# Half of each product with B moved to GpSimd behind a ScalarE copy, and all four batches in one straight block

## The reference, cut to what matters

```
def step(h, ts):
    dt, B_t, C_t, x_t = ts
    dA = jnp.exp(A[None] * dt[:, :, None])
    dBx = dt[:, :, None] * B_t[:, None, :] * x_t[:, :, None]
    h = dA * h + dBx
    y = jnp.einsum('bdn,bn->bd', h, C_t) + D * x_t
    return (h, y)
...
y = y * jax.nn.silu(z)
y = y @ out_proj_w.T + out_proj_b
r = y + residual
```

## Time and profile before

| | |
|---|---|
| median of 3 runs | 2946.02 us (2938.42 to 2959.98) |
| the profiled execution | 2938.01 us, span 2936.2 us |
| scan stage, first ScalarE instruction of the block to the last residual | 1283.7 to 1622.4 us, 338.7 us |
| busy in the whole span | PE 76%, DVE 60%, ACT 35%, POOL 23% |
| mean granted TensorE clock | 0.845 of full speed |

### The profile page before, as it was taken

How to read it: one execution, slowest core, us unless ns; L and a number is a source line. 1 busy time by engine, 2 the same in 40 slices (tenths; PEclk the granted TensorE clock), 3 DMA queues, 4 the chain that set the end, 5 groups by cost and what they waited for, 6 DMA issues and landing times. The chain is left out here.

```text
span 2936.2 us, 37724 instructions
## 1 busy us (share of the span) xinstructions
PE 2233.7 (76%) x12210; PEld 1461.8 (50%) x12210; DVE 1761.6 (60%) x4110; ACT 1034.3 (35%) x2220; POOL 687.5 (23%) x1221
## 2 busy tenths in 40 slices
PE   2579699995999784546666599398489868999688
PEld 1245588882555444212222355287334346776577
DVE  2546566674675455789898554554689655556422
ACT  0135222220564451444343134322157723344222
POOL 0033244431110420124354232134111000000121
PEclk8669799996796797778788589599779979999799
DMA  7032000003110410000000321000411000000000
GB/s 282 0 99 52 1 1 0 0 0 100 44 51 15 106 40 0 0 0 0 0 0 0 110 49 35 1 1 0 136 37 44 23 36 1 0 0 0 1 0 14
DMA packets 58426, 93.92 MB, mean 32 GB/s; under 512 B 11264, under 2 KB 31040, under 8 KB 57152
## 3 DMA queue, kind: packets, MB, share of 16 engines
q0 software_dynamic: 29952, 36.45, 5.1%
q1 hardware_dynamic: 27488, 45.67, 4.7%
q10 hardware_dynamic: 864, 10.30, 0.9%
HBM read 65.63 MB, written 31.29 MB: 33 GB/s over the span
## 5 line engine op out<-in xcount | busy, mean ns | idle before, releaser
L815 DVE TENSOR_REDUCE m<-bank 128x1 f32<-128x512 f32 (+3 forms) x512 | 272.4, 583 | 77.4 <-PE bank L968 50.2
L1235 DVE TENSOR_REDUCE m<-bank 128x2 f32<-128x308 f32 x384 | 164.3, 475 | 203.8 <-PE bank L1507 118.1
L2322 PEld LDWEIGHTS bank<-w_ffn,eh 128*128 128x128 f32 x2144 | 276.5, 191 | 20.0
L2322 PE MATMUL bank<-w_ffn,eh 128*128 128x128 f32 x2144 | 278.7, 275 | 0.0
L2311 PE MATMUL bank<-x_hi,w_hi 128*128 x472 | 217.3, 460 | 71.0 <-POOL w_lo L2239 55.0
L936 ACT ACTIVATE p<-bank 128x512 f32<-128x512 f32 (+3 forms) x512 | 234.0, 522 | 97.6 <-PE bank L1014 58.7
L2661 PE MATMUL bank<-hc,w_start 128*128 128x512 f32 x256 | 162.0, 766 | 102.7 <-POOL hc L2609 102.6
L2592 DVE TENSOR_TENSOR_SCAN sh<-dA,dbx 128x512 f32<-128x512 f32 x128 | 218.2, 1743 | 2.2
L966 PE MATMUL bank<-K,Qf 32*128 32x512 f32 (+2 forms) x512 | 180.8, 507 | 37.9 <-PEq L330 33.1
L2237 POOL CAST w_hi<-w_ffn 128x256 fp32r<-128x256 f32 (+1 forms) x256 | 95.0, 371 | 482.3 <-SPq L2227 325.1
L2609 POOL TENSOR_TENSOR hc<-sh,cb 128x1024 f32<-128x1024 f32 x64 | 152.1, 2377 | 199.9 <-DVE sh L2592 151.0
(11 more groups left out here) (399 smaller groups left out, 4587.5 us busy)
## 6 DMA issues: line engine op xcount, KB each, us to landing
Qf<-stack_q_plain POOLq DMA_DIRECT2D x48, 256.0 KB, 3.0
Qf<-stack_q_masked POOLq DMA_DIRECT2D x32, 256.0 KB, 3.0
K<-stack_k_self POOLq DMA_DIRECT2D x32, 256.0 KB, 3.1
w_ffn<-ffn_dram ACTq DMA_DIRECT2D x1, 6144.0 KB, 33.5
stack_q_plain<-q_hi SPq DMA_DIRECT2D x24, 256.0 KB, 3.4
stack_q_masked<-q_hi SPq DMA_DIRECT2D x16, 256.0 KB, 3.0
stack_k_self<-k_hi SPq DMA_DIRECT2D x16, 256.0 KB, 3.1
K<-stack_k_ctx POOLq DMA_DIRECT2D x48, 80.0 KB, 2.6
```

Source lines behind the costliest of these rows:

```text
L815: ins = dve.reduce_max(k.m[:, t, h:h + 1], bank[:, 0:(t + 1) * P if k.kind == "page" else S], AX)
L1235: dve.reduce_max(k.m[:, t:t + 2, h], first_banks[c % 3][:].rearrange("p (a k) -> p a k", a=2)[:, :, 0:S2], AX).then_inc(sem("max_done"), 1)
L2322: last = pe.matmul(bank[:, t * P:(t + 1) * P], k.h[:, n % RING, t * P:(t + 1) * P], w(down.format(e))[:, i * P:(i + 1) * P], start=(i == 0 ...
```

## The change

- dbx is cut in two. VectorE makes half 0 (L2590 of the changed kernel), GpSimd makes half 1 (`second_dbx`, L2615). Both read B from a new SBUF tile bb, double buffered, which ScalarE copies from the bank (`copy_B`, L2638). TensorE's next spread into a B bank waits for that copy, no longer for dbx.
- VectorE's second scan of a step waits for GpSimd's half. GpSimd issues `second_dbx(u + 2)` behind the product hc of step u. ScalarE issues `copy_B(u + 1)` ahead of the two exponentials of step u.
- dtx is double buffered by batch and made at step 8 of the batch before (`weigh`, two 512-column products).
- The loop is gone: one straight block of 64 steps over all four batches.

```diff
-        self.dtx = sb("dtx", [P, 2, S])
+        self.dtx = sb("dtx", [P, 2, 2, S])
+        self.bb = sb("bb", [P, 2, S])
...
-    steps = BODY * NSTATE
+    steps = B * NSTATE
...
+            def weigh(e):
+                for i in range(2):
+                    last = dve.tensor_tensor(k.dtx[:, e % 2, i], k.xc[:, e, i], k.dt[:, e], ALU.mult)
+                last.then_inc(sem("dtx_ready"), 1)
+                dve.wait_ge(sem("dtx_ready"), e + 1)
+
+            weigh(0)
             for u in range(steps):
                 e, s = divmod(u, NSTATE)
-                if s == 0:
-                    dt = k.dt[:, bass.ts(b0 + e, 1), :]
-                    xc = k.xc[:, bass.ts(b0 + e, 1)].rearrange("p o i q -> p (o i) q")
-                    ch.link(dve.tensor_tensor(k.dtx[:], xc, dt.to_broadcast([P, 2, S]), ALU.mult))
-
-                dve.wait_ge(sem("B_done"), u + 1)
-                dve.tensor_tensor(k.dbx[:, u % 2], k.dtx[:], over(ps[u % 2][:], 1, 2), ALU.mult).then_inc(sem("dbx_ready"), 1)
-                dve.wait_ge(sem("dbx_ready"), u + 1)
+                if s == 8 and e + 1 < B:
+                    weigh(e + 1)
+
+                dve.wait_ge(sem("B_ready"), u + 1)
+                dve.tensor_tensor(k.dbx[:, u % 2, 0], k.dtx[:, e % 2, 0], k.bb[:, u % 2], ALU.mult).then_inc(sem("first_dbx"), 1)
+                dve.wait_ge(sem("first_dbx"), u + 1)
                 for i in range(2):
+                    if i == 1:
+                        dve.wait_ge(sem("second_dbx"), u + 1)
                     dve.wait_ge(sem("dA_ready"), 2 * u + i + 1)
...
         @block.gpsimd
         def _(pool):
+            def second_dbx(u):
+                e = u // NSTATE
+                if u % NSTATE == 0:
+                    pool.wait_ge(sem("dtx_ready"), e + 1)
+                pool.wait_ge(sem("B_ready"), u + 1)
+                nc.gpsimd.tensor_tensor(k.dbx[:, u % 2, 1], k.dtx[:, e % 2, 1], k.bb[:, u % 2], ALU.mult).then_inc(sem("second_dbx"), 1)
+
+            second_dbx(0)
+            second_dbx(1)
             for u in range(steps):
...
                 nc.gpsimd.tensor_tensor(k.hc[:, u % 2], k.h[:, u % 2], over(k.cb[:, u % 2], 1, 2), ALU.mult).then_inc(sem("hc_ready"), 1)
+                if u + 2 < steps:
+                    second_dbx(u + 2)
...
+            def copy_B(u):
+
+                act.wait_ge(sem("B_done"), u + 1)
+                if u >= 2:
+                    act.wait_ge(sem("first_dbx"), u - 1)
+                    act.wait_ge(sem("second_dbx"), u - 1)
+                nc.scalar.copy(k.bb[:, u % 2], ps[u % 2][:]).then_inc(sem("B_ready"), 1)
+
+            copy_B(0)
             for u in range(steps):
                 e, s = divmod(u, NSTATE)
+                if u + 1 < steps:
+                    copy_B(u + 1)
...
                 if u >= 2:
-                    pe.wait_ge(sem("dbx_ready"), u - 1)
+                    pe.wait_ge(sem("B_ready"), u - 1)
...
-            with nc.Fori(0, B // BODY, 1) as i:
-                scan_block(net, i * BODY, k)
+            scan_block(net, k)
             scan_finish(net, k)
```

More of the change, by code:

```diff
@@ L53 @@
 LN_BN = 6
-BODY = 2
 GROUP = 4
@@ L2548, in scan_prepare, with scan_block @@
     end_of_block(net)
-def scan_block(net, b0, k):
+def scan_block(net, k):
     nc, sem, ps, w = net.nc, net.sem, net.ps, net.w
-    steps = BODY * NSTATE
+    steps = B * NSTATE
     with nc.Block() as block:
@@ L2567, in apply_gate @@
                 for i in range(2):
-                    last = dve.tensor_tensor(k.g[:, i], ps[4 + 2 * (e % 2) + i][:], k.zs[:, bass.ts(b0 + e, 1), i].rearrange("p o q -> p (o q)"), ALU.mult)
+                    last = dve.tensor_tensor(k.g[:, i], ps[4 + 2 * (e % 2) + i][:], k.zs[:, e, i], ALU.mult)
                 last.then_inc(sem("gated_ready"), 1)
@@ L2573, in residual @@
                 dve.wait_ge(sem("out_done"), e + 1)
-                xn = k.n.xn[:, bass.ts(b0 + e, QT), :]
+                xn = k.n.xn[:, e * QT:(e + 1) * QT, :]
                 dve.tensor_tensor(xn, ps[4 + 2 * (e % 2)][:].rearrange("p (t d) -> p t d", t=QT), xn, ALU.add).then_inc(sem("r_ready"), 1)
+            def weigh(e):
[4 more added lines that the diff above has]
+            weigh(0)
             for u in range(steps):
                 e, s = divmod(u, NSTATE)
-                if s == 0:
-                    dt = k.dt[:, bass.ts(b0 + e, 1), :]
-                    xc = k.xc[:, bass.ts(b0 + e, 1)].rearrange("p o i q -> p (o i) q")
-                    ch.link(dve.tensor_tensor(k.dtx[:], xc, dt.to_broadcast([P, 2, S]), ALU.mult))
-                dve.wait_ge(sem("B_done"), u + 1)
-                dve.tensor_tensor(k.dbx[:, u % 2], k.dtx[:], over(ps[u % 2][:], 1, 2), ALU.mult).then_inc(sem("dbx_ready"), 1)
-                dve.wait_ge(sem("dbx_ready"), u + 1)
+                if s == 8 and e + 1 < B:
[3 more added lines that the diff above has]
+                dve.wait_ge(sem("first_dbx"), u + 1)
                 for i in range(2):
+                    if i == 1:
+                        dve.wait_ge(sem("second_dbx"), u + 1)
                     dve.wait_ge(sem("dA_ready"), 2 * u + i + 1)
@@ L2596, in _ @@
                     residual(e - 1)
-            apply_gate(BODY - 1)
-            residual(BODY - 1)
-            dve.wait_ge(sem("r_ready"), BODY)
+            apply_gate(B - 1)
+            residual(B - 1)
+            dve.wait_ge(sem("r_ready"), B)
         @block.gpsimd
         def _(pool):
+            def second_dbx(u):
[6 more added lines that the diff above has]
+            second_dbx(1)
             for u in range(steps):
@@ L2609, in _ @@
                 nc.gpsimd.tensor_tensor(k.hc[:, u % 2], k.h[:, u % 2], over(k.cb[:, u % 2], 1, 2), ALU.mult).then_inc(sem("hc_ready"), 1)
+                if u + 2 < steps:
+                    second_dbx(u + 2)
+            pool.wait_ge(sem("hc_ready"), steps)
         @block.scalar
         def _(act):
+            def copy_B(u):
[5 more added lines that the diff above has]
+            copy_B(0)
             for u in range(steps):
                 e, s = divmod(u, NSTATE)
+                if u + 1 < steps:
+                    copy_B(u + 1)
                 for i in range(2):
@@ L2618, in _ @@
                         act.wait_ge(sem("h_ready"), 2 * (u - 2) + i + 1)
-                    dt = k.dt[:, bass.ts(b0 + e, 1), :].rearrange("p o q -> p (o q)")
-                    nc.scalar.activation(k.dA[:, u % 2, i], dt, ACT.Exp, scale=k.A[:, i * NSTATE + s:i * NSTATE + s + 1]).then_inc(sem("dA_ready"), 1)
+                    nc.scalar.activation(k.dA[:, u % 2, i], k.dt[:, e], ACT.Exp, scale=k.A[:, i * NSTATE + s:i * NSTATE + s + 1]).then_inc(sem("dA_ready"), 1)
                 act.wait_ge(sem("C_done"), u + 1)
@@ L2630, in spread @@
                 e, s = divmod(u, NSTATE)
-                bc = k.bc[:, bass.ts(b0 + e, S)]
+                bc = k.bc[:, e * S:(e + 1) * S]
                 if u >= 2:
-                    pe.wait_ge(sem("dbx_ready"), u - 1)
+                    pe.wait_ge(sem("B_ready"), u - 1)
                 pe.matmul(ps[u % 2][:], w("sel")[:, s * P:(s + 1) * P], bc, start=True, stop=True).then_inc(sem("B_done"), 1)
@@ L2657, in _ @@
                     for i in range(2):
-                        pe.matmul(ps[4 + 2 * (e % 2) + i][:], k.D[:, i, :], k.xc[:, bass.ts(b0 + e, 1), i].rearrange("p o q -> p (o q)"), start=True, stop=False)
+                        pe.matmul(ps[4 + 2 * (e % 2) + i][:], k.D[:, i, :], k.xc[:, e, i], start=True, stop=False)
                 pe.wait_ge(sem("hc_ready"), u + 1)
@@ L2664, in _ @@
                     output(e - 1)
-            output(BODY - 1)
+            output(B - 1)
     end_of_block(net)
```

## The result

The changed kernel takes 3020.76 us (median of 4 runs, 3005.65 to 3024.09) against 2942.22 us before; the ratio is 1.0249 with an interval of 1.0189 to 1.0309. Five further rounds of the same kernel gave 1.0262 (1.0240 to 1.0284), the narrower figure; one of their six executions took 5126 us, which nothing on record explains, and is left out of that ratio. The changed kernel is slower, as forecast, and lies 7 us under the predicted 3028 us, inside the range of 3000 to 3065.

A forecast was written before the change was run, and what follows sets the result against it. VectorE instructions with two SBUF operands and GpSimd products were taken to exclude each other, bounding the step. Terms +95.8 − 15.2 + 1.7 + 2.4 + 1.5 = +86.2 us gave 3024 or 3032; forecast 3028, range 3000 to 3065.

The forecast's parts named there:

- The exclusive chain: Scan stage step: scans, GpSimd products and VectorE's dbx half run one after another, 6.2 us taken against 4.68, +95.8 us.
- the first sum: Scan stage step, VectorE's scans and GpSimd taking turns: 1.08 + 1.06 + 1.08 + 0.61 + 2.21, together 6.04 us.
- rival 1: Scan stage step: instructions exclude each other for whole recorded durations, joints cost extra; 6.61 us, total 3054; chance 0.20.
- ScalarE's copy: Scan stage: 64 more copies of B, 37.5 us more on ScalarE, covered by the longer step; cost 0.
- The seam: Between the loop's blocks: GpSimd's 17.50 us idle gap turns into an ordinary batch change, −15.2 us.
- Batch changes: Residuals waiting for TensorE's projection: three at 3.5 us each, 10.5 − 8.8 = +1.7 us.
- dtx: Scan stage: three pairs of 512-column VectorE products, all in the exclusive chain, 4.1 − 1.7 = +2.4 us.
- The start: Before the first hc: the copy of B and one or two GpSimd halves come first, about +1.5 us.
- The tail: After the last hc of the scan stage: the same as before, 0.
- Rivals 3: Scan stage step about 3.7 us, 512-column pieces slipping past or only scans and long products excluded; 2870 us; chance 0.04.
- rival 4: Scan stage: second_dbx falls into VectorE's idle or waiting time, step near 5.4 us, total 2980; chance 0.05.

The follow-up runs named there:

- idle_product: straight plus one more 512-column GpSimd product of two SBUF tiles behind each hc, read by nobody; 5.71 us a step, 2987.7 us in one run.
- whole_from_copy: straight plus ScalarE's copy of B, with VectorE making all of dbx from that SBUF copy; 5.52 us a step, 2991.1 us in one run.
- idle_memset: idle_product with GpSimd's extra product replaced by a write-only memset of 1280 columns; 4.68 us a step, 2929.7 us in one run.
- copy_unused: straight plus ScalarE's copy of B, waited for but not read, dbx still from PSUM; 4.68 us a step, some 5.4; 2935.2 us in one run.
- straight: The kernel before with only the loop removed, all four batches in one block; ratio 0.9973, 4.68 us a step.
- split_hc: straight with hc halved: VectorE makes half 0 reading C from PSUM, GpSimd half 1; ratio 0.9827, 2893.7 us, 4.08 us a step.

## Why the prediction was right, step by step

- **The exclusive chain** was right: 6.04 us by turns was worked out, 6.01 is measured, and idle_product and whole_from_copy show it as the cause, with idle_memset and copy_unused as their controls. I took 6.2, allowing for orders with fewer shortened joints. Scan and GpSimd alternate in every steady step, so the first sum was the right one; no steady step shows the other order. 63 × 0.19 = 12 us of the forecast's excess is this.
- **The two parts of the loss.** GpSimd's second product is 1.02 us a step (4.68 to 5.70), VectorE's move to the copy 0.31 (to 6.01). The move alone, whole and without the extra product, is 0.84.
- **Held whole** (rival 1, 6.61 us) fell: the joints overlap by 0.1 to 0.2 us each, so whole recorded durations overstate the step by 0.6.
- **ScalarE's copy** at 0 was right for this kernel, and the slack was as narrow as worked out. The exponential was put at 5.7 us after the end of the hc before; in the closest steady steps the scan is dispatched 5.6 us after it, 0.41 us ahead of its turn. By the same 0.41 us a step below about 5.6 us (an estimate, 6.01 − 0.41) would begin to pay for it, and copy_unused and some steps of whole_from_copy do.
- **The seam**, −15.2, and with the batch change in its place about −10: measured −9.7 in straight.
- **Batch changes:** three residuals cost 10.0 us in the first profile, 10.5 were forecast. That they agree so well is in part luck: single ones were 5.34, 3.17 and 1.48, and in the second profile the three are 3.12, 1.48 and 4.02, 8.6 in all. **dtx:** 3 × 1.37 = 4.1, as forecast. **The start:** first dtx to first hc 6.52 us against 5.00, +1.5 as forecast. **The tail** was forecast at 0 and is +1.3: TensorE has a granted clock of 0.73 in the stage instead of 0.82, and its last four hc records take 3.78 us, not 1.98.
- The stage by terms: 63 × 1.33 = 83.8 for the step, −15.2 seam, +2.4 dtx, +1.2 residuals, +1.0 for gates (0.35 each), −1.0 in the last step, which has no half product behind it, +1.5 start, +1.3 tail: 75.0, against 86.2 forecast.
- **Rivals 3 and 4** (faster, or the turns only partly paid) fell with the step of 6.01 us. The sum of rival 4 was off by a little: +45 − 9.6 on the same base of 2942 gives 2977, not 2980.
- **Luck in the total.** From the profiled 2938.0 us the forecast worked out 3024, and the profiled execution took 3024.09. That is chance: the stage took 11 us less than forecast, and 11 us that the forecast put at nothing lie outside it. The fair comparison is 75 us in the stage against 86, and 77 to 79 us in the medians.

## What to carry to other kernels

Before work goes to GpSimd beside VectorE, ask of each VectorE instruction whether both its operands lie in SBUF: in these traces, all of fp32 products and scans, those took turns with every GpSimd product that read SBUF, and the ones with an operand in PSUM did not. Copying an operand out of PSUM to share it can so turn a free instruction into one on the chain. The gain lies the other way: let VectorE take its part straight from PSUM, and keep GpSimd's reading pieces short enough to lie under it.

## What the runs showed of the hardware

- A scan along time (`TENSOR_TENSOR_SCAN`, two SBUF operands) takes turns with GpSimd's products as a plain product does: 1.19 us alone, up to 3.25 us recorded when it waits.
- In the steady steps turns alternate: behind hc came the waiting scan, not GpSimd's next product. This need not be a rule of alternation. In each steady step of the changed kernel the scan was dispatched 0.37 us or more before GpSimd's next product, so first come, first served gives the same order, and no run tells the two apart.
- A VectorE product of 1024 columns costs the same from two SBUF tiles as with one operand in PSUM, 1.19 us.
- GpSimd's duration in the profile includes its wait: 1.27 us without one, 2.17 us behind a scan, for the same 512 columns.
- TensorE's mean granted clock in the scan stage followed the step, with the same 496 matmul records each time: 0.73 of full speed at 6.01 us a step, 0.77 at 5.71 (idle_product), 0.82 at 4.68 and 0.92 at 4.08 (split_hc). The four records of one hc took 3.77 us in many steps and 1.98 in others.
